# A rehearsal that counts the measured issue time of every SyncE transfer

## The reference, cut to what matters

```
x = x + 0.5 * L0_ffn(layernorm(x))    # FP4-quantised gated FFN, 256 -> 704 -> 256
x = x + L0_attn(layernorm(x))         # decayed linear attention, sigmoid q and k
x = x + 0.5 * L0_ffn(layernorm(x))
x = x + 0.5 * L1_ffn(layernorm(x))    # soft mixture: 1024 slots, dispatch and combine softmax
x = x + L1_attn(layernorm(x))         # causal softmax attention, 16 heads of 16, LoRA weights
x = x + 0.5 * L1_ffn(layernorm(x))
```

```
q, k, v = (lora_linear(x, ...) split in 16 heads of 16)
scores = where(causal, q @ k.T / 4, -inf);  attn = softmax(scores)
out = lora_linear(attn @ v)
```

```
logits = xn @ se.T                         # 512 x 1024 for each batch
slots = softmax over experts(logits).T @ xn ;  h = gelu(slots @ w1) ; processed = h @ w2
out = softmax over all slots(logits) @ processed
```

## Time and profile before

| | |
|---|---|
| median of 3 runs | 2572.69 us (2568.84 to 2573.86) |
| profiled execution, its own time | 2571.66 us |
| its span, first to last instruction | 2569.9 us |
| mean granted TensorE clock | 0.965 |
| busy: PE, DVE, ACT, POOL | 90%, 73%, 65%, 34% |
| SyncE: DMAs of a1Q and a1K by line 724 | 96 and 96 |

### The profile page before, as it was taken

One profiled execution on the slowest core, in us unless ns is written; L12 is line 12 of the kernel. 1 busy time (PEld: TensorE's weight loads), 2 busy tenths in 40 slices (PEclk: granted clock), 3 DMA queues, 4 the chain that ended last, 5 costly groups with the idle time before them and its releaser, 6 DMA issues.

```text
span 2569.9 us, 54204 instructions
## 1 busy us (share of the span) xinstructions
PE 2314.0 (90%) x22616; PEld 1777.8 (69%) x22616; DVE 1878.7 (73%) x3184; ACT 1668.6 (65%) x2917; POOL 885.6 (34%) x631
## 2 busy tenths in 40 slices
PE   2889889889989898999899899999989898899999
PEld 2566566657777776767687677677667676687788
DVE  8689889998787967777777686868776776552631
ACT  4377666647676674776766767476575748685666
POOL 0122222222413322462534535353463526332122
PEclk7899999999999999999999999999999999999999
DMA  5000000000000000000000000000000000000000
GB/s 177 19 1 1 1 1 1 1 1 1 1 1 1 1 1 26 2 26 2 14 14 2 26 2 16 12 14 14 23 14 10 16 20 2 10 2 9 9 10 9
DMA packets 34979, 33.05 MB, mean 13 GB/s; under 512 B 7664, under 2 KB 34096, under 8 KB 34736
## 3 DMA queue, kind: packets, MB, share of 16 engines
q1 hardware_dynamic: 34736, 29.60, 3.5%
HBM read 12.54 MB, written 4.19 MB: 7 GB/s over the span
## 4 chain that ended last, share of the span: by engine, by line
PE 66%; DVE 20%; ACT 5%; issue 4%; POOL 2%; SPq 2%; DMA 1%; DVEq 0%; ACTq 0%
PE psum L749 17%; PE psum L751 16%; PE psum L750 15%; PE psum L755 6%; PE psum L1186 2%; PE psum L1037 2%; PE psum L1188 2%; PE psum L1187 2%; PE psum L1090 2%; PE psum L1067 2%; SPq L724 1%; POOL a1pr L2181 1%; DVE a1pr L1943 1%; DVE f0hT L1810 1%; PE psum L1017 1%
## 5 line engine op out<-in xcount | busy, mean ns | idle before, releaser
L2194 POOL TENSOR_TENSOR f1hT<-f1g,f1hT 128x512 f16<-128x512 f32 x256 | 308.9, 1211 | 655.1 <-ACT f1hT L1596 654.4
L2181 POOL TENSOR_TENSOR a1pr<-a1PT,a1pr 128x1024 f16<-128x1024 f32 (+1 forms) x176 | 357.5, 2033 | 302.9 <-DVE a1pr L1943 302.8
L749 PE MATMUL psum<-f1w2h,f1hT 128*128 128x256 f16 x1024 | 282.9, 276 | 8.8 <-issue 7.3
L749 PE MATMUL psum<-f1sl,f1w1h 128*128 128x256 f16 x1024 | 282.2, 276 | 9.5 <-ACT f1g L1591 7.6
L751 PE MATMUL psum<-f1w2h,f1hT 128*128 128x256 f16 x1024 | 282.2, 276 | 0.0
L750 PE MATMUL psum<-f1w2l,f1hT 128*128 128x256 f16 x1024 | 282.1, 275 | 0.0
L750 PE MATMUL psum<-f1sl,f1w1h 128*128 128x256 f16 x1024 | 281.2, 275 | 0.0
L751 PE MATMUL psum<-f1sl,f1w1l 128*128 128x256 f16 x1024 | 281.0, 274 | 0.0
L1920 DVE TENSOR_REDUCE a1nm<-psum 128x2 f32<-128x768 f32 (+3 forms) x176 | 198.1, 1126 | 84.8 <-PE psum L1017 83.9
L1943 DVE CAST a1pr<-a1PT 128x1024 f16<-128x1024 f32 (+1 forms) x176 | 167.9, 957 | 80.6 <-ACT a1PT L1493 58.2
L2170 POOL TENSOR_TENSOR f0h<-f0Y,f0sc 128x704 f32<-128x704 f32 x64 | 93.2, 1457 | 342.3 <-DVE f0Y L1798 342.3
(11 more groups left out here) (339 smaller groups left out, 6835.2 us busy)
## 6 DMA issues: line engine op xcount, KB each, us to landing
a1Q<-a1st SPq DMA_DIRECT2D x96, 64.0 KB, 2.6
a1K<-a1st SPq DMA_DIRECT2D x96, 64.0 KB, 2.6
x<-in_L_attn_x SPq DMA_DIRECT2D x8, 512.0 KB, 7.8
out<-x SPq DMA_DIRECT2D x8, 512.0 KB, 3.0
wslot<-in_L_ffn_w SPq DMA_DIRECT2D x1, 1024.0 KB, 9.5
wraw<-in_L_ffn_w SPq DMA_DIRECT2D x1, 1024.0 KB, 5.6
wslot<-in_L_ffn_slot_embeds SPq DMA_DIRECT2D x1, 1024.0 KB, 7.9
a1Q<-a1mr SPq DMA_DIRECT2D x64, 4.0 KB, 1.7
```

The lines of the kernel that those rows point to most:

```text
L749: e.matmul(out, lh, rh, start=start, stop=False)
L2181: e.tensor_tensor(a1["pr"][:, i % 2, 1, :, 0:w], a1["PT"][:, i % 2, :, 0:w], a1["pr"][:, i % 2, 0, :, 0:w], ALU.subtract).then_inc(s["a1_pl"])
L2194: e.tensor_tensor(hT1[:, c % 2, 1, 2 * hp:2 * hp + 2, :], gg[:, hp % 2, :, :], hT1[:, c % 2, 0, 2 * hp:2 * hp + 2, :], ALU.subtract).then_ ...
```

## The change

One number in the rehearsal's cost table: SyncE is taken to be occupied for 635 ns by the issue of a DMA instead of 60 ns. The transfer's own time in the rehearsal (1000 ns, the bytes, 1000 ns) stays, counted from an issue that now comes later for each DMA behind the first. In the built program every instruction, buffer, bank and wait of before is there again, in another order on each engine.

```diff
@@ -265,7 +265,7 @@
         return self.vec(out)
 
     def dma_start(self, out, src, **kw):
-        return self.note(60, None, out.shape[0] * self.each(out) * (2 if out.dtype == mybir.dt.float16 else 4))
+        return self.note(635, None, out.shape[0] * self.each(out) * (2 if out.dtype == mybir.dt.float16 else 4))
```

## The result

The changed kernel takes 2516.07 us (median of 4, 2512.75 to 2518.56) against 2573.06 of the kernel before (median of 4): the ratio is 0.978, with a 95% interval of 0.976 to 0.980. The profiled executions stand 54 us apart (spans 2569.9 and 2515.7).

What follows compares the result with a forecast made beforehand. TensorE was taken as the bound from about 600 us on, with VectorE's order counting in f0 and a0. The terms sum to -21.5 us, two thirds counted as -14.5: 2558 us forecast, 8-in-10 range 2537 to 2584.

Steps and rivals of the forecast that it cites:

- a new draw of the order: In f0 and a0, 100 to 600 us: changed fine order moves the time 12 us up or down; 0 in the sum.
- worse rival: The new order is worse in f0 and a0, with as much again lost in the middle by collisions; chance 0.22.
- terms 2 and 3: The clock, -5 us, and the rest of a1 on TensorE, -4, -2 and +1 us.
- The argument for 0: Batches leave blocks after the same share of work in both orders, so no stage gains or loses by its place.
- Term 1, the copies: Middle: longer leads cut TensorE's waits for copies into a1Q and a1K from 21.3 to 10.8 us, -10.5; bounds 0 and -21.3.
- Term 2, the clock: Around four copy waits: half of 11.4 us of lost full-speed time comes back, -5 us; bounds 0 and -11.
- the four places: Four waits for copies with the granted clock between its levels, 0.67 to 0.83, losing 11.4 us of full-speed time.
- Term 3: Rest of a1 on TensorE: a1pr wait -4 us, readers of banks 0 and 1 -2, f1's second product +1.
- Term 4, the start: Start: f0xh is turned in TensorE's idle time before a1's last weights land, -1 us; bounds +3 and -6.
- The sum's two thirds: Other TensorE waits stand close behind in the middle, so two thirds of -21.5 us count, -14.5.
- The worse draw: 100 to 600 us, VectorE bound: pieces put ahead of their inputs; with 25 us lost the time is 2583; chance 0.22.
- more than counted: All of terms 1 to 3 lands and the f0 draw is kind by 12 us: 2538; chance 0.13 for over 22 us gained.

Runs made afterwards that it cites:

- cut60: Order of the kernel before kept, but from batch 1 on one of six copies of each Q and K half issued: 2554.0 us against 2572.24 beside it.
- cut635: Order of the changed kernel kept, but from batch 1 on one of six copies of each Q and K half issued: 2511.49 us against 2516.07.
- cut_rest: Order of only_rest kept, but from batch 1 on one of six copies of each Q and K half issued: 2570.42 us against 2591.65.
- only_rest: Kernel before with 635 ns counted for every transfer but the copies into a1Q and a1K, which stay at 60: 2591.65 us.
- d635_act: Changed kernel (issue cost 635) with ScalarE's signal lag in the rehearsal at 131 ns instead of 130: 2536.27 us.

## Why the prediction was wrong, step by step

The direction was right, and so was the middle as the place of the copies' gain, but the size was wrong by a factor of four. The prediction had a step that it called a new draw of the order and put at 0 in the sum and 12 us up or down in the range, in f0 and a0. That step failed: with the copies out of the way the two orders are 42.5 us apart. One draw scatters by 15.5 us (standard deviation), so the difference of two draws by 22, and the scatter is mostly in the middle (16 and 14 us), where the prediction put none outside its worse rival, and less in f0 and a0 (9 and 5 us to the point at 660 us of work, which is passed at about 820 us). The 12 us ahead of the middle were as large as the allowance; what had no place in the sum or the range was most of the 45 - 13 = 32 us in the middle, of which terms 2 and 3 had forecast 10. The argument for 0, that every batch leaves a block after the same share of work, did not bear on it: the time is in the fine order within the blocks. A range that holds 8 in 10 had to reach about 28 us (1.28 x 22, an estimate) to each side for the draw alone. That this draw was kind, and so kind, is luck.

- **Term 1, the copies: right.** -10.5 us forecast, 21.3 to 8.2 = -13.1 read in the profiles, and 10 to 14 us as cut60 and cut635 price it. The counted leads gave most of the pattern: 10.8 us left against 8.2, none above 1 us at batches 1 to 4 for Q. Batches 5 and 6 kept 1.7 and 1.4 us instead of 2.3 and 2.8, and batch 7 had 1.7 for 0.9. Not forecast were 1.3 and 1.1 us for K at batches 3 and 7, and the 3.5 us for K at batch 0 were not there. That the new cost still falls 1.4 us short of the trace is seen too: with 1000 the waits are 0 and 1.6 us.
- **Term 2, the clock: right at the four places, not in the sum.** The whole kernel gets about 20 us of full-speed time back (1 - 0.965 of 2569.9 is 90, 1 - 0.972 of 2515.7 is 70), and TensorE's busy time falls by 13.4, more than the 5 forecast and than the 11.4 of the four places. But it isn't the copies' waits that bring it. cut60 took them away: of the 11.4 us lost at the four places 7.9 came back, and the mean was 0.964 for 0.965, so as much was lost elsewhere. cut635 has 0.971 for 0.972. Only in cut_rest did the mean rise, from 0.959 to 0.964. So for the two orders of this case the term comes to nothing as a part of the copies' effect, and the clock that came back belongs to the draw.
- **Term 3: the sum right in sign, its parts not.** a1pr, forecast at -4 by the shortfall of its distances, went from 9.5 to 9.8. The readers of banks 0 and 1, forecast at -2, went from 12.8 + 10.6 to 8.9 + 3.6: -10.9. Of the counted distances only the one whose need was read from the trace place by place gave its wait.
- **Term 4, the start: as forecast,** and worth little; what it gave at 130 us (3 us ahead) was lost again at 206 (2 us behind the kernel before, at equal work).
- **The sum's two thirds: not borne out.** A third was taken off because the next wait might swallow what is gained. Few of the waits were swallowed: 42.1 us of them gave 44.0 of time and 38.0 of TensorE's idle time.
- **The rivals.** The worse draw did not come here, but it is real: only_rest, one number away, is at 2591.65. What came was its mirror, the case called more than counted, 22 us beyond the 2538 that it was given: it had a kind draw of 12 us in f0 and a0 and none in the middle. VectorE's busy time between 100 and 600 us, the sign of the worse draw, hardly moved (449.9 and 450.9).

One reading of the rows was wrong and cost nothing: "no single wait is large" holds for the copies' stage, but at the start TensorE waits once for 19.8 us for the first weights (18.1 in the kernel after).

What stays open: of the 26 us between the two kinds of draws, 12 go through the waits for the copies (16.5 against 4.8). The other 14, with an error of 8, may be a real effect of the cost on the order in the middle, or still the scatter; 17 draws don't settle it. Nor was it tried to name the pieces that make the changed kernel's order 24 us better than the mean of its own kind.

## What to carry to other kernels

Where a search orders the program, any edit to its tables is two things at once: the effect that it is meant to have and a new draw. Measure the scatter first, with edits that mean nothing, and judge the edit by several draws, or by the wait that it should shorten; one pair of times, however precise, tells little (here the 57 us between the two kernels hold 13 us of waits, and the two kinds of orders are 26 us apart in the mean). To price a wait, keep the order and shorten what is waited for. And with such scatter, trying eight or nine draws and keeping the best is itself worth something: the best of each kind here is 24 us under the mean of its kind.

## What the runs showed of the hardware

The sixth copy at the place of the earlier trace rows, in SyncE's timeline of the kernel before, and its time from issue to landing in us (the last number):

```profile
1098.59 0.59 SPq L724 DMA_DIRECT2D a1Q<-a1st  x1
a1Q<-a1st SPq DMA_DIRECT2D x1, 64.0 KB, 3.2
```

It is issued 3.5 us after the first (1095.06) and lands 3.2 us later, at 1101.78; TensorE goes on at 1101.82. In cut60 the one copy there is issued at 1095.02 and lands 2.6 us later, 4.2 us earlier than the sixth, where the expectation of cut60 had counted 3.3. The 2.6 us of the earlier trace rows count from the start of the issue. A copy into a1Q and the next into a1K start 0.63 us apart, so the 635 ns are the distance of two issues (0.59 of the row and 0.04 between). The mean clock stayed where it was (0.965 and 0.964) when TensorE's idle time fell by 18 us in cut60: the dips behind the waits went or shrank, and others opened elsewhere in the middle. Two executions of one program can differ by 0.009 in the mean clock and by 13 us in time (d635_act).
